# Holding each quad's load back until the quad three ahead of it has landed, in steps 5 to 12 of a graph-network layer

## The chip, the cores and the metric

One core of one Trainium2 chip runs the program. The metric is the device time of one execution in microseconds (us), and lower is better. The kernel before takes 317.98 us (median of 3 runs, 317.53 to 318.19).

## The reference

The kernel computes one pre-norm graph layer over 12,500 nodes of 128 features and 200,000 edges of 128 features, all in 32-bit floats. The edges come sorted by `dst`.

```python
h = jnp.maximum(_layernorm(x, axis=-1), 0.0)
agg = jax.ops.segment_sum(edge_attr, dst, num_segments=x.shape[0])
h = jnp.concatenate([h, agg], axis=-1)
h = jax.nn.relu(h @ W1 + b1)
h = jax.nn.relu(h @ W2 + b2)
h = h @ W3 + b3
# layer norm of h over its features, times ln_w, plus ln_b
x = x + h
```

The edge features are 102.4 MB of the 109.9 MB that are read from HBM, and each is used once.

## The kernel before, in words

**Edges.** The 200,000 rows are cut into 130 quads of 1,536 rows (`QUAD`, 768 KB each) and a small tail. A quad lies in one of the 8 slots of the tile `ring` (`RING = 8`; quad q in slot q mod 8). `load_quad` (L295) loads it with two DMAs of 384 KB, both of which raise the slot's own semaphore `edges_loaded[slot]`, by 32 in total (`LANDED`). TensorE (PE) sums a quad with 24 matmuls (`seg`, L438), which wait for that semaphore and raise `seg_done` when they are through. ScalarE copies the sums, a second matmul puts them at the right nodes (L449, with a placement matrix from GpSimd, L800), and VectorE adds them into `agg` (L954).

**Nodes.** The nodes are 32 groups of 384 and a last one of 212. One *step* i of the pipeline handles four quads (4i+6 to 4i+9) and one group's three layers. The `x` rows of group i+3 are loaded in SyncE's step i by `load_x` (L290, 192 KB).

**The order of the loads.** SyncE (SP) issues all loads of edges and x and nearly all stores, in one written order, on one DMA queue. In its step i it loads x of group i+3 and then the quads 4i+14 to 4i+17. Each goes through `reload`, which waits until the slot's previous quad has been summed:

```python
def reload(q, slot):
    sp.wait_ge(seg_done, q - RING + 1)
    load_quad(q, slot)
```

Steps 1 to 12 run in one loop over pairs of steps (L347), steps 13 to 28 in a second (L350) in which the first eight groups' results are also stored in parts (L322). After the last quad's load the other groups are stored, two at a time (L327), and the program ends with the last group's layers and stores (L758, L309, L314).

Of the kernel before, what the change touches and what calls it, by code (L numbers as in the profile page):

```python
# [39 lines left out]
LANDED = 2 * 16  # L40
# [17 lines left out]
RING = 8  # L58
# [10 lines left out]
TRIPLES = BLOCKS * BLOCK // 3 + 2  # L69
XAHEAD = 3  # L70
AHEAD = 6
OUT_PARTS = ((0, 48), (48, 96), (96, P))
STEPS = GROUPS - 1
ROUNDS = (STEPS - 3) // 2
STORED_EARLY = 8
WTS = 6 * 16


def gnn_kernel(nc, x, dst, edges, w1, b1, w2, b2, w3, b3, lnw, lnb, out):
    assert GROUPS == 32 and QUADS == 4 * STEPS + AHEAD and LAST_P * LAST_PER == LAST_N and RC * RP == REST  # L80
    with ExitStack() as ctx:
        def sb(name, shape, dt=F32):
            return ctx.enter_context(nc.sbuf_tensor(name, shape, dt))

        def sem(name):
            return ctx.enter_context(nc.semaphore(name))
# [16 lines left out]
        turn = sb("turn", [P, ROWT])  # L103
# [3 lines left out]
        row_at = sb("row_at", [P, QUADS + 1])  # L107
        rows_at = sb("rows_at", [P, AHEAD])
        excess = sb("excess", [P, 5])
# [72 lines left out]
        edges_loaded = [sem(f"edges_loaded{k}") for k in range(RING)]  # L182
# [6 lines left out]
        added = sem("added")  # L189


        dve_went_on = sem("dve_went_on")
        pool_went_on = sem("pool_went_on")

# [77 lines left out]
        with nc.Block() as block:  # L272
# [3 lines left out]
            def _(sp):  # L276
# [9 lines left out]
                def load_x(g, par, before):  # L286

                    if not (isinstance(before, int) and before == 0):
                        sp.wait_ge(x_loaded[par], 16 * before)
                    sp.dma_start(xg(g), group_rows(x, g)).then_inc(x_loaded[par], 16)  # L290

                def load_quad(q, slot):

                    for k in range(2):
                        sp.dma_start(ring_slot(slot)[:, k * HALF:(k + 1) * HALF, :], half_of_edges(q, k)).then_inc(edges_loaded[slot], 16)  # L295
# [11 lines left out]
                def store(g):  # L307
                    sp.wait_ge(out_ready, g + 1)
                    sp.dma_start(group_rows(out, g), xg(g)).then_inc(stored, 16)  # L309

                def store_last(count):
                    sp.wait_ge(out_ready, count)
                    for p0, p1 in LAST_PARTS:
                        sp.dma_start(last_rows(out, p0, p1), xg(LAST)[p0:p1, :]).then_inc(stored, 16)  # L314

                def store_part(g, k):

                    p0, p1 = OUT_PARTS[k]
                    if k == 0:
                        sp.wait_ge(out_ready, g + 1)  # L320
                    rows = out[bass.ds(g * CHUNK + p0 * PER, (p1 - p0) * PER), :]
                    sp.dma_start(rows.rearrange("(p j) f -> p (j f)", j=PER),  # L322
                                 xs[p0:p1, bass.ds(g * CHUNK, CHUNK)]).then_inc(stored, 16)

                def store_two(g):
                    sp.wait_ge(out_ready, g + 2)
                    sp.dma_start(out[bass.ds(g * CHUNK, 2 * CHUNK), :].rearrange("(g p j) f -> p g (j f)", p=P, j=PER),  # L327
                                 xs[:, bass.ds(g * CHUNK, 2 * CHUNK)].rearrange("p (g e) -> p g e", g=2)).then_inc(stored, 16)
# [5 lines that stand above are left out]
                def fast():  # L334
                    for q in range(RING, RING + AHEAD):
                        reload(q, q % RING)

                    def step(i, par, pairs, g=None, parts=()):

                        load_x(i + XAHEAD, (par + XAHEAD) % 2, pairs + (par + XAHEAD) // 2)  # L340
                        for k in range(4):
                            reload(4 * i + RING + AHEAD + k, (4 * par + AHEAD + k) % RING)
                            if k in parts:
                                store_part(g, parts[k])

                    step(0, 0, 0)
                    with sp.Fori(0, ROUNDS - STORED_EARLY) as t:  # L347
                        step(2 * t + 1, 1, t)
                        step(2 * t + 2, 0, t + 1)
                    with sp.Fori(ROUNDS - STORED_EARLY, ROUNDS) as t:  # L350
                        g = t - (ROUNDS - STORED_EARLY)
                        step(2 * t + 1, 1, t, g, {0: 0, 3: 1})
                        step(2 * t + 2, 0, t + 1, g, {2: 2})
                    sp.wait_ge(seg_done, QUADS - RING + 1)
                    tail = QUADS % RING
                    sp.dma_start(ring[:, tail, 0:PER * D],
                                 edges[TAIL0:EDGES, :].rearrange("(p j) f -> p (j f)", j=PER)).then_inc(edges_loaded[tail], 16)
                    pairs = (GROUPS - 2 - STORED_EARLY) // 2
                    for k in range(pairs):
                        store_two(STORED_EARLY + 2 * k)  # L360
                    for g in range(STORED_EARLY + 2 * pairs, GROUPS - 1):
                        store(g)
                    store_last(GROUPS)
                    singles = GROUPS - STORED_EARLY - 2 * pairs
                    sp.wait_ge(stored, 16 * (len(OUT_PARTS) * STORED_EARLY + pairs + singles + len(LAST_PARTS)))

                def general():
# [26 lines left out]
                    sp.wait_ge(stored, 16 * (GROUPS + len(LAST_PARTS)))  # L394

                branch(sp, fast, general)


            @block.tensor
            def _(pe):  # L400
# [110 lines left out]
                def fast():  # L511
                    pe.wait_ge(wts_loaded, WTS)
                    for q in range(AHEAD):
                        if q >= 2:
# [6 lines left out]
                    def step(i, par, pairs):  # L521


                        for k in range(4):
                            turn_q = 4 * par + AHEAD + k
                            q = 4 * i + AHEAD + k
# [660 lines left out]
```

## Time and profile before

| what | value |
|---|---|
| median of 3 runs | 317.98 us |
| the profiled execution: its own time | 318.58 us |
| its span, first to last instruction | 316.8 us |
| PE, DVE, ACT, POOL busy | 86%, 78%, 47%, 56% |
| mean granted TensorE clock | 0.984 |
| moved by DMA | 116.50 MB, mean 368 GB/s |

The profiled execution's own time is 1.8 us above its span, and 0.6 us above the median of the runs shown. PE is TensorE, DVE VectorE, ACT ScalarE, POOL GpSimd, SP SyncE; SPq and ACTq are the queues from which these engines issue DMAs. The time of an SPq row is the time that the issue took on SyncE, not that of the transfer. In the windows view the DMA share is the busy share of the core's 16 DMA engines; the records of neighbouring packets overlap, so that a full queue reads 1.06.

### The profile page before, as it was taken

What the parts mean: (1) busy time and instruction counts of PE and PEld (TensorE: products, weight loads), DVE (VectorE), ACT (ScalarE), POOL (GpSimd) and SP (SyncE); (2) the same over time, 40 slices, a digit from 0 to 9 for tenths busy, and PEclk for the clock granted to TensorE, in tenths of its full rate; (3) what the DMA queues carried; (4) which work ended last, traced back from release to release, by engine and by line L of the source; (5) the groups of instructions that cost most, each with busy time, mean ns of one, the idle gap of its engine ahead of it and who ended that gap; (6) DMA issues with size and microseconds to landing.
All of it is one profiled execution on the core that took longest, in us unless ns stands there. A gap on an engine that the chain in (4) does not pass through costs nothing.

```text
span 316.8 us, 12734 instructions
## 1 busy us (share of the span) xinstructions
PE 271.7 (86%) x3927; PEld 185.0 (58%) x3927; DVE 246.4 (78%) x944; ACT 149.6 (47%) x407; POOL 179.0 (56%) x208
## 2 busy tenths in 40 slices
PE   2949998998998888888988888889888888898991
PEld 0726666665665566655665565656655656565570
DVE  4946588989787878877787888778777887878885
ACT  1442555555544445455444454554443545544632
POOL 8636555566555656655555656555556565555431
PEclk9978999999999999999999999999999999999998
DMA  7999999999999999999999999999999999999994
GB/s 245 343 380 371 372 373 372 373 373 373 373 373 373 373 374 373 373 373 373 378 381 378 382 380 379 379 383 379 380 381 379 382 381 380 380 383 380 383 397 153
DMA packets 81855, 116.50 MB, mean 368 GB/s; under 512 B 5712, under 2 KB 81840, under 8 KB 81840
## 3 DMA queue, kind: packets, MB, share of 16 engines
q1 hardware_dynamic: 80826, 115.86, 103.2%
q10 hardware_dynamic: 1014, 0.46, 0.5%
q8 instruction: 7, 0.11, 0.1%
q14 instruction: 8, 0.07, 0.1%
HBM read 109.90 MB, written 6.40 MB: 367 GB/s over the span
## 4 chain that ended last, share of the span: by engine, by line
SPq 55%; PE 14%; issue 12%; DMA 11%; DVE 6%; ACT 0%; DVEq 0%; POOL 0%; POOLq 0%
SPq L295 43%; DMA ring<-in_edge_attr 9%; PE part_ps L438 6%; SPq L322 5%; SPq L290 5%; PE place_ps L449 3%; DMA dst_i<-in_dst 1%; PE hid_ps L466 1%; SPq L331 1%; PE hid_ps L483 1%; PE hid_ps L473 1%; PE y_ps L489 1%; DVE onehot L878 1%; DVE local L900 1%; DVE least L898 1%
## 5 line engine op out<-in xcount | busy, mean ns | idle before, releaser
L800 POOL TENSOR_SCALAR place<-iota,rows_at 128x128 f32<-128x128 f32 x131 | 104.9, 804 | 104.2 <-PE place_ps L449 95.0
L438 PE MATMUL part_ps<-ring,onehot 128*32 128x128 f32 x3120 | 113.4, 279 | 26.7 <-DMA ring<-in_edge_attr 25.8
L438 PEld LDWEIGHTS part_ps<-ring,onehot 128*32 128x32 f32 x3120 | 78.4, 110 | 72.6 <-issue 50.1
L954 DVE TENSOR_TENSOR agg<-place_ps,agg 128x128 f32 x131 | 38.0, 290 | 50.8 <-PE place_ps L449 49.0
L449 PE MATMUL place_ps<-place,part 128*128 128x128 f32 (+1 forms) x262 | 64.4, 328 | 2.6 <-POOL place L800 2.3
L808 POOL TENSOR_TENSOR xs<-xs,vecs 128x384 f32 (+2 forms) x33 | 54.8, 1662 | 19.4 <-ACT h L669 19.4
L878 DVE TENSOR_TENSOR onehot<-iota,local_t 128x768 f32<-128x768 f32 x66 | 63.5, 963 | 0.3 <-issue 0.3
L655 ACT ACTIVATE part<-part_ps 128x128 f32<-128x128 f32 x131 | 35.0, 268 | 48.4 <-PE part_ps L438 46.8
L449 PEld LDWEIGHTS place_ps<-place,part 128*128 128x128 f32 (+1 forms) x262 | 39.8, 190 | 29.1 <-issue 22.1
L669 ACT ACTIVATE h<-xs,x_shift,x_rstd 128x128 f32 (+2 forms) x98 | 41.3, 483 | 2.4 <-DVE x_shift L871 2.4
L685 ACT ACTIVATE hid<-hid_ps,b1s 128x384 f32<-128x384 f32 (+1 forms) x33 | 19.0, 577 | 45.4 <-PE hid_ps L473 45.4
L1013 DVE SCALAR_TENSOR_TENSOR xs<-z,y_rstd,xs 128x128 f32 (+1 forms) x93 | 32.5, 400 | 4.1
L489 PE MATMUL y_ps<-w3s,hid 128*128 128x128 f32 x192 | 29.8, 291 | 0.0
L661 ACT ACTIVATE x_std<-x_mv,eps 128x3 f32<-128x3 f32 (+1 forms) x33 | 9.8, 296 | 41.1 <-DVE x_mv L859 41.1
L995 DVE SCALAR_TENSOR_TENSOR z<-y,y_mv,vecs 128x128 f32<-128x128 f32 x96 | 28.9, 355 | 0.1
L678 ACT ACTIVATE h_t<-ht_ps 128x384 f32<-128x384 f32 x32 | 22.3, 696 | 13.6 <-PE ht_ps L458 13.6
L483 PE MATMUL hid_ps<-hid,w2s 128*128 128x384 f32 (+1 forms) x66 | 26.8, 487 | 0.5 <-ACT hid L685 0.5
L466 PE MATMUL hid_ps<-h_t,w1x 128*128 128x384 f32 x64 | 26.1, 489 | 0.8 <-ACT h_t L678 0.8
L473 PE MATMUL hid_ps<-agg,w1a 128*128 (+2 forms) x66 | 26.5, 483 | 0.0
L489 PEld LDWEIGHTS y_ps<-w3s,hid 128*128 128x128 f32 x192 | 23.8, 191 | 1.4 <-issue 0.5
L851 DVE BATCH_NORM_STATS2 x_stats<-xs 128x6 f32 (+2 forms) x98 | 22.0, 279 | 1.0 <-DVE flag_i L940 0.8
L979 DVE BATCH_NORM_STATS2 y_stats<-y 128x6 f32<-128x128 f32 x96 | 20.8, 272 | 0.1
(86 smaller groups left out, 201.9 us busy)
## 6 DMA issues: line engine op xcount, KB each, us to landing
ring<-in_edge_attr SPq DMA_DIRECT2D x260, 384.0 KB, 8.8
xs<-in_x SPq DMA_DIRECT2D x32, 192.0 KB, 8.5
out_x<-xs SPq DMA_DIRECT2D x11, 384.0 KB
out_x<-xs SPq DMA_DIRECT2D x16, 72.0 KB
dst_i<-in_dst SPq DMA_DIRECT2D x1, 768.0 KB
out_x<-xs SPq DMA_DIRECT2D x8, 48.0 KB
ring<-in_edge_attr SPq DMA_DIRECT2D x1, 192.0 KB, 8.7
out_x<-xs SPq DMA_DIRECT2D x1, 192.0 KB
```

The costliest lines, as they stand in the source:

```text
L295: sp.dma_start(ring_slot(slot)[:, k * HALF:(k + 1) * HALF, :], half_of_edges(q, k)).then_inc(edges_loaded[slot], 16)
L438: last = nc.tensor.matmul(part_ps[par_q % 2][s * WIN:(s + 1) * WIN, 0:D], onehot[:, oct_par, first + s, j, :], e[:, s, j * D:(j + 1) * D], ...
L449: nc.tensor.matmul(place_ps[par_q % 2][:, 0:P], part[0:rows, par_q % 2, :], place[0:rows, par_q % 2, :], start=True, stop=True).then_inc(p ...
L483: nc.tensor.matmul(hid2_ps[:, 0:n], w2s[:, :], hid1[:, 0:n], start=True, stop=True).then_inc(hid2_done, 1)
L489: last = nc.tensor.matmul(y_ps[:, j * D:(j + 1) * D], hid2[:, j, :], w3s[:, :], start=True, stop=True)
L655: nc.scalar.activation(part[0:rows, par_q % 2, :], part_ps[par_q % 2][0:rows, 0:D], ACT.Copy).then_inc(part_copied, 1)
L669: last = nc.scalar.activation(h[0:rows, j, :], xg(g, j), ACT.Relu, bias=x_shift[0:rows, j:j + 1], scale=x_rstd[0:rows, j:j + 1])
L800: nc.gpsimd.tensor_scalar(place[:, par_q % 2, :], iota[:, 0:P], rows_at[:, k:k + 1], None, ALU.is_equal).then_inc(place_ready, 1)
L808: nc.gpsimd.tensor_tensor(v, v, lnbs[0:rows, :].unsqueeze(1).to_broadcast([rows, per, D]), ALU.add).then_inc(x_biased, 1)
L878: nc.vector.tensor_tensor(onehot[:, par % 2, :, :, :], iota[:, 0:WIN].unsqueeze(1).unsqueeze(1).to_broadcast([P, OCT, PER, WIN]), local_t[ ...
L954: nc.vector.tensor_tensor(v, place_ps[par_q % 2][:, 0:P], v, ALU.add).then_inc(added, 1)
L1013: last = nc.vector.scalar_tensor_tensor(xg(g, j), z_of(g, j), r[0:rows, j:j + 1], xg(g, j), ALU.mult, ALU.add)
```

## The change

In SP's step, `few_underway` is called ahead of each of the four `reload`s when the step is built with `level=True`. It waits until quad q-3, counted from the quad q that is about to be loaded, has landed in full, and then raises a semaphore `sp_went_on`, for which nobody waits. The loop over steps 1 to 12 is cut in two: steps 1 to 4 as before, steps 5 to 12 with `level=True`. Everything else stays.

```diff
+UNDERWAY = 3
+LEVEL_FROM = 2
...
+        sp_went_on = sem("sp_went_on")
...
+                    def few_underway(turn, pairs):
+
+                        n = turn - UNDERWAY
+                        sp.wait_ge(edges_loaded[n % RING], LANDED * (pairs + n // RING + 1))
+                        sp.sem_inc(sp_went_on, 1)
+
-                    def step(i, par, pairs, g=None, parts=()):
+                    def step(i, par, pairs, g=None, parts=(), level=False):
 
                         load_x(i + XAHEAD, (par + XAHEAD) % 2, pairs + (par + XAHEAD) // 2)
                         for k in range(4):
+                            if level:
+                                few_underway(4 * par + RING + AHEAD + k, pairs)
                             reload(4 * i + RING + AHEAD + k, (4 * par + AHEAD + k) % RING)
...
-                    with sp.Fori(0, ROUNDS - STORED_EARLY) as t:
+                    with sp.Fori(0, LEVEL_FROM) as t:
                         step(2 * t + 1, 1, t)
                         step(2 * t + 2, 0, t + 1)
+                    with sp.Fori(LEVEL_FROM, ROUNDS - STORED_EARLY) as t:
+                        step(2 * t + 1, 1, t, level=True)
+                        step(2 * t + 2, 0, t + 1, level=True)
```

On SyncE's queue, the first half of an odd step in the loop over steps 1 to 12 before the change. `x_loaded_even` is raised by x loads, `seg_done` by PE; ISA and REGISTER_ALU rows are SyncE's own short instructions.

```order
L347 UNCONDITIONAL_BRANCH
L347 ISA
L290 ISA [waits x_loaded_even]
L290 REGISTER_ALU
L290 DMA xs<-in_x 128x384
L331 ISA
L295 ISA [waits seg_done]
L295 DMA ring<-in_edge_attr 128x2x384
L295 ISA
L295 DMA ring<-in_edge_attr 128x2x384
```

The same place of the loop over steps 5 to 12 after the change, and the start of the next quad. `edges_loaded7` and `edges_loaded0` are raised by the loads of the slots 7 and 0.

```order
L361 UNCONDITIONAL_BRANCH
L361 ISA
L293 ISA [waits x_loaded_even]
L293 REGISTER_ALU
L293 DMA xs<-in_x 128x384
L344 REGISTER_ALU
L334 ISA [waits edges_loaded7]
L298 ISA [waits seg_done]
L298 DMA ring<-in_edge_attr 128x2x384
L298 ISA
L298 DMA ring<-in_edge_attr 128x2x384
L344 ISA
```

The order of the DMAs is the same. New is the wait on the semaphore of an earlier quad's slot, ahead of the wait on `seg_done`, with two short instructions for it. Both DMAs of the quad, and all that SyncE issues later, stand behind it. The other four engines' instructions are those of before.

## Rows read from the trace of the kernel before

**Rows 1.** The page's 40 slices of the span: DMA share, and what the DMA engines moved.

```profile
DMA  7999999999999999999999999999999999999994
GB/s 245 343 380 371 372 373 372 373 373 373 373 373 373 373 374 373 373 373 373 378 381 378 382 380 379 379 383 379 380 381 379 382 381 380 380 383 380 383 397 153
```

**Rows 2.** Windows: steps without stores, steps with them.

```profile
core 0: us, PE busy (x) PEld busy (x) DVE busy (x) ACT busy (x) POOL busy (x), PEclk, DMA share, GB/s
60.00:148.00 88.00, 79.95 (x1199) 54.59 (x1201) 72.02 (x283) 44.18 (x122) 52.73 (x61) 1.00 1.06 373
150.00:290.00 140.00, 123.57 (x1843) 83.98 (x1843) 110.95 (x432) 66.56 (x183) 81.22 (x95) 1.00 1.06 380
```

**Rows 3.** Waits of PE, 60 to 148 us: in total, times, longest.

```profile
PE part_ps L438 <- DMA ring<-in_edge_attr: 8.0, 8, 1.0
```

**Rows 4.** Waits of SyncE's queue, whole span.

```profile
SPq L295 <- PE part_ps L438: 3.8, 6, 1.1
```

**Rows 5.** Timeline of SyncE's queue: start, duration; the x loads of steps 4, 5, 6, 12 and 13.

```profile
67.36 0.76 SPq L290 DMA_DIRECT2D xs<-in_x  x1
68.43 7.60 SPq L295 DMA_DIRECT2D ring<-in_edge_attr  x8
76.76 0.36 SPq L290 DMA_DIRECT2D xs<-in_x  x1
77.44 7.30 SPq L295 DMA_DIRECT2D ring<-in_edge_attr  x8
84.97 1.39 SPq L290 DMA_DIRECT2D xs<-in_x  x1
...
139.03 0.76 SPq L290 DMA_DIRECT2D xs<-in_x  x1
140.11 7.60 SPq L295 DMA_DIRECT2D ring<-in_edge_attr  x8
148.33 0.36 SPq L290 DMA_DIRECT2D xs<-in_x  x1
```

**Rows 6.** Line L295 at 60 to 148 us: issue durations (ns), issue to landing.

```profile
L295 SPq DMA_DIRECT2D ring<-in_edge_attr x80: 372/718/1484, 59.7 to 146.9; - x80
DMA to landing us min/median/max: 7.4/9.0/10.1
```

**Rows 7.** The same of L295 at 150 to 290 us and at 0 to 20 us.

```profile
DMA to landing us min/median/max: 7.0/8.8/10.5
...
DMA to landing us min/median/max: 4.7/9.7/11.3
```

**Rows 8.** Chain of waits around quad 58: start, duration.

```profile
131.21 0.04 issue
131.28 0.04 issue
131.32 0.37 SPq L295
131.70 0.04 issue
131.74 0.05 SPq L295
131.79 0.04 issue
131.86 0.04 issue
131.90 9.52 DMA ring<-in_edge_attr
```

**Rows 9.** Timeline and chain at the program's start, when the queues are empty.

```profile
0.74 0.44 SPq L278 DMA_DIRECT2D dst_i<-in_dst  x1
...
1.73 4.25 DMA dst_i<-in_dst
```

**Rows 10.** Timeline of PE, steps without stores: start, busy, idle before.

```profile
78.83 0.86 PE L438 MATMUL part_ps<-ring,onehot 128*32 128x128 f32 x24 [0.97 <-DMA ring<-in_edge_attr]
```

**Rows 11.** Windows of 2 us, columns as in rows 2.

```profile
16.00:18.00 2.00, 0.18 (x8) 0.00 (x0) 0.99 (x12) 0.88 (x2) 0.00 (x0) 1.00 1.06 386
140.00:142.00 2.00, 0.96 (x21) 0.72 (x24) 1.86 (x7) 0.82 (x2) 1.72 (x3) 1.00 1.06 373
156.00:158.00 2.00, 2.00 (x35) 1.68 (x34) 1.66 (x7) 1.76 (x6) 1.23 (x2) 1.00 1.06 388
160.00:162.00 2.00, 2.00 (x22) 0.99 (x15) 1.83 (x6) 0.28 (x1) 1.74 (x2) 1.00 1.06 372
```

**Rows 12.** DMA queues of the page: packets, MB, share of 16 engines.

```profile
q8 instruction: 7, 0.11, 0.1%
q14 instruction: 8, 0.07, 0.1%
```

## The prediction

> **What bounds the kernel now.** I read the page's slices first. The DMA engines show 9 tenths or more in every slice but the first and the last, and the rate stands at 373 GB/s through the slices in which steps 5 to 12 lie, then near 380 [rows 1]. The windows say the same with more figures: share 1.06, the reading of a full queue, and 373 GB/s between 60 and 148 us, while PE is busy for 79.95 of 88 us, DVE, ACT and POOL for less, at full granted clock [rows 2]. PE waits only for edges there: 8 times in 88 us, 8.0 us in all [rows 3], once per step, as at 78.83 us [rows 10]. So the pace of a step is that of its bytes. SyncE's timeline gives it: x loads at 76.76 us (step 5) and 148.33 us (step 13), 71.57 us for 8 steps, 8.95 us a step [rows 5]. A step moves 4 quads of 768 KB and 192 KB of x, 3,264 KB or 3.34 MB; at 373 GB/s that is 8.96 us. A quad alone is 0.786 MB and takes 2.11 us.
>
> Next, what holds SyncE back. In the whole span it waited for PE (a slot not free) 3.8 us in 6 places [rows 4]. That is not what spaces its issues. An issue takes 372 ns when nothing stops it and 718 ns in the median [rows 6]; eight of them and the x load fill about 8.4 of the 8.9 us of a step [rows 5]. The queue itself is full and holds the issue. The depth that follows from this: quad 58's halves were issued at 131.32 and 131.90 us, and the second landed 9.52 us later, at 141.42 [rows 8]. From the first issue that is 10.1 us, and 10.1 us at 373 GB/s is 3.77 MB, or 4.5 quads with their share of x. Between four and five quads are therefore underway before the change.
>
> **The change part by part.**
>
> *The new wait.* A quad q is issued when q-3 has landed, so at most two quads, q-2 and q-1, lie ahead of it instead of about four. SyncE's position slips towards the landings, from 10.1 us ahead to about three quads, 3 x 2.11 = 6.3 us (with one x load in four quads, 6.7 us on average): some 3.5 us less in store. Landings are what PE waits for, and they move only if the queue runs dry. When q-3 has landed, 2 quads or 4.2 us of work are still queued. In this time SyncE has to get past its wait and the first bytes of q have to come. SyncE's part: two or three short instructions at 0.04 to 0.08 us each, as between the rows of the chain [rows 8], say 0.3 us, and 0.37 us for the first half's issue. The rest no row shows by itself, so I bound it. From above: at the program's start, with all queues empty, 780 KB of `dst` were issued from 0.74 us on and had landed in full at 5.98 us [rows 9]. That is 5.24 us, of which the bytes take 2.14 us at 373 GB/s, so at most 3.1 us are start and completion together, the issue among them. With SyncE's 0.3 us that makes 3.4 us, against a cover of 4.2 us. From below it is the bare issue, 0.7 us. Take the upper value: 0.8 us of cover is left, and the queue does not run dry. Cost 0. If the 16 DMA engines are not level with each other, the semaphore follows the slowest, and an engine that is ahead may idle for a moment. It had its share done early, and the slowest, whose landing everybody waits for, still has its 4.2 us.
>
> By the Trainium skill (DMA: Bandwidth & Descriptors, Bandwidth and Anatomy of one DMA) a transfer costs a fixed time of about 2.0 us and then its bytes. The trace's bound of 3.1 us is larger and fits it from above; by the page's figure, an estimate, 1.9 us of cover would be left instead of 0.8. Its rule for kernel authors, to issue a DMA early and wait for it late, speaks against this change, but costs nothing here as long as that cover holds.
>
> *What is queued behind the wait.* On SyncE the x load of the next step, the other quads, and from step 13 on the first stores. Their order on the DMA queue stays word for word, so x of group i+3 still lands ahead of quad 4i+14, and VectorE gets it in the same turn. Nothing else waits for SyncE.
>
> *SyncE's own time.* It loses 8.4 us of blocked issuing per step and gets back a wait in its place. Eight issues of 0.37 us, the x load's 0.36 us and some 4 x 0.4 us of short instructions are 4.9 us of 8.95. SyncE does not become the bound.
>
> *The way in and out.* At step 5 it pauses once for about 3.5 us while the store of queued loads shrinks. At step 13 the wait ends and four free slots let it issue faster than the data land (0.37 + 0.2 us a half, against 1.05 us), so the queue fills again. Both lie beside a queue that stays busy. Cost 0.
>
> *Does a shorter queue move bytes faster?* This is where a gain could be. Within the trace of before the depth varies and the rate does not follow it. At 60 to 148 us halves land 7.4 to 10.1 us after issue, at 373 GB/s [rows 2, 6]. At 150 to 290 us they land in 7.0 to 10.5 us [rows 7], yet a window in which no store was in flight shows 372 GB/s [rows 11]. The 380 of that stage comes from windows with stores in them, such as 388 at 156 us. The one fast stretch of loads alone, 386 GB/s at 16 us, came with the deepest queue (up to 11.3 us to landing) and with compute engines nearly idle [rows 7, 11]. I take no gain.
>
> The sum is 0. The profiled execution's 316.8 us of span and 318.58 us stay as they are, and so does the median of the runs, 317.98, on which I forecast: 318.0 us.
>
> **The rivals.**
>
> *Loads run faster with less in flight.* For it: the rate is not at its ceiling, since 380 and 386 GB/s occur [rows 2, 11], and the steps in question are those with the fullest queue. Against it: the evidence above. Price: 8 steps of 3.34 MB take 71.6 us at 373 GB/s, 70.3 at 380 and 69.2 at 386, so 1.3 us, at most 2.4. Result 316.7, at the outside 315.6. The Trainium skill (DMA: Bandwidth & Descriptors, Latency and other measured facts) holds that HBM answers in 0.2 us on average and in 2 us at high load; a shorter queue would be lighter load. No row here shows latency falling with depth.
>
> *The DMA engines draw level.* If some lag behind the others, as landings that are counted by the slowest would hide, a hold that leaves the leaders idle could give the laggards a larger share of HBM, and every later quad would land earlier. The rows do not show single engines. The gain would be at most the lag that is made good: even at the rate of 380 against 373 (1.9%) over 71.6 us, 1.3 us again. It ends at the same place, 316.7. Gain and condition are close to the first rival's, and I count them together.
>
> *The queue runs dry.* The place is the wait on `edges_loaded` in each of the 32 quads. If SyncE's restart and the start of a transfer last longer than 4.2 us, three quads take that time plus their own 2.11 us instead of 6.3 us, so each us too much costs a third of a us per quad, 10.7 us in all. Against it: the bound of 3.4 us. For it: that bound comes from a core at rest, and a loaded memory may answer later; the nearest loaded rows, 7.0 us at the least to landing, contain queueing that can't be told from latency [rows 7]. From 4.2 us on it decides. At 4.5 us the result is 318.0 + 3.2 = 321.2, at 4.3 us 319.1. The far end, if the 10.1 us of quad 58 were all latency, would be (10.1 + 0.3)/3 = 3.5 us a quad instead of 2.2, +40 us; since 10.1 us is just what the 4.5 queued quads need, I leave it out.
>
> *More program to fetch.* SyncE's program grows by some 51 instructions, and another piece of it may have to be fetched through a DMA engine. The seven pieces of queue 8 are 0.11 MB, 16 KB each [rows 12]; one DMA engine moves a sixteenth of 373 GB/s, so a piece holds its engine for 0.7 us. If that is the engine that lands last, all later quads come 0.7 us later: 318.7. If it is not, nothing changes.
>
> **How the numbers follow.** No change: 0.54. Faster loads or level engines: 0.25. Queue runs dry: 0.11. A fetch on the last engine: 0.10. A measurement of this kernel tells no less than about 0.2% (0.6 us) from no change. Both kinds of the slower side end beyond that, if the fetch only just, so 0.21 slower, 0.54 same, 0.25 faster. The range goes from the first rival's 316.7 to 319.1, the small end of a dry queue; the far ends of both sides (under 316.7, over 319.1) keep the 2 in 10.
>
> **What would show it.** In the changed profile: the rate and share at 80 to 148 us (373 and 1.06 if I am right; 376 or more for the first rivals; below 370 and a share under 1.06 for a dry queue). Issue to landing of L298 there should fall from 9.0 to about 5.5 to 6 us, and its issues to the bare 0.37 us; if it stays at 9, the change does not do what it says. SyncE should wait for `ring` DMAs some 32 times. PE's waits for edges should stay one per step, about 1 us. The x load of step 13 should be issued about 3.5 us later than at 148.33 us while the landings stay where they were. I would be wrong if the pace of landings depended on how the queue is filled, in either direction.

## The result, and the profile after

The changed kernel takes 319.38 us (median of 11 runs, 318.20 to 320.74) against 318.09 us (11 runs, 317.53 to 318.84) of the kernel before. The ratio is 1.0036, 95% interval 1.0022 to 1.0049: about 1.1 us slower. A second set of 12 runs gave 1.0031 (1.0011 to 1.0051). The forecast was no change, 318.0 us, with a range up to 319.1.

The profiled execution took 318.53 us, at the low end of its kernel's runs, while that of before (318.58) lay at the high end of its own. Both spans are 316.8 us, so the spans show nothing, and the loss has to be read from stretches. First the page's slices, DMA share and GB/s.

```profile
DMA  7999999999999999999999999999999999999995
GB/s 251 327 378 377 372 374 374 373 374 373 368 367 368 370 374 373 373 373 373 377 380 378 381 381 379 379 384 378 378 383 379 379 379 382 379 381 380 380 398 185
```

Against [rows 1] four slices in the held steps fall below 373 GB/s: 368, 367, 368 and 370. They cover 79 to 111 us, the first three to four of the eight held steps. Then the rate is that of before. The windows (window in us, its length, busy time and count of each engine, granted clock, DMA share, GB/s):

```profile
core 0: us, PE busy (x) PEld busy (x) DVE busy (x) ACT busy (x) POOL busy (x), PEclk, DMA share, GB/s
84.00:100.00 16.00, 14.20 (x213) 9.89 (x213) 12.93 (x47) 7.81 (x22) 9.87 (x11) 1.00 1.04 365
100.00:116.00 16.00, 14.23 (x212) 9.86 (x212) 13.52 (x54) 8.14 (x23) 10.27 (x12) 1.00 1.06 374
116.00:148.00 32.00, 28.95 (x443) 19.62 (x441) 25.34 (x104) 16.20 (x45) 17.37 (x22) 1.00 1.06 373
160.00:280.00 120.00, 105.42 (x1576) 71.58 (x1574) 94.80 (x370) 57.26 (x157) 69.22 (x80) 1.00 1.06 380
```

The share of 1.04 where a full queue reads 1.06 says that some DMA engines had nothing to do between 84 and 100 us. 8 GB/s of 373 over 16 us is 0.34 us of moving. At 116 to 148 us, with the hold still on, share and rate are full, as in [rows 2].

SyncE does what was forecast. Its queue's waits over the whole span (in total, times, longest), its line L298 (L295 before) at 80 to 148 us, and its timeline at steps 5 and 13:

```profile
SPq L345 <- DMA ring<-in_edge_attr: 27.4, 29, 3.7
...
SPq L298 <- PE part_ps L452: 3.8, 6, 1.2
```

```profile
L298 SPq DMA_DIRECT2D ring<-in_edge_attr x62: 372/373/373, 81.0 to 147.9; - x62
...
DMA to landing us min/median/max: 4.0/5.4/6.0
```

```profile
76.42 0.36 SPq L293 DMA_DIRECT2D xs<-in_x  x1
80.96 7.71 SPq L298 DMA_DIRECT2D ring<-in_edge_attr  x8
...
151.59 0.36 SPq L293 DMA_DIRECT2D xs<-in_x  x1
```

It waits 29 times for landings, 3.7 us the first time; every issue takes the bare 0.37 us, where the median was 718 ns [rows 6]; a half lands 5.4 us after its issue instead of 9.0; the x load of step 13 goes out 3.3 us later than in [rows 5]. PE's waits for edges at 60 to 148 us look like those of [rows 3]:

```profile
PE part_ps L452 <- DMA ring<-in_edge_attr: 8.0, 9, 1.0
```

**The 16 DMA engines one by one.** A quad's landing is in the trace as 32 single events, two for each of the 16 engines (every engine carries a sixteenth of each half and reports it). No view above shows them. Worked out from the trace, for some quads, the times in us of the first event, the average of the 32, and the last, for which PE waits; levelled engines would have first and last 1.05 us apart, a half's own time:

```
               quad 33              quad 66                quad 129
before         80.97  82.66  85.02  155.28 156.95 159.26   297.06 299.10 301.88
after          81.06  82.70  84.80  156.26 157.44 158.62   298.00 299.74 301.76
```

Before the change first and last are 4.0 us apart: some engines are 3 us ahead of the slowest and stay so. Over the held stretch, quad 33 to 66, the average landing takes 74.74 us instead of 74.28: 0.46 us lost. But the last landing takes 73.81 instead of 74.24: it comes 0.4 us *sooner*. After the hold, to quad 129, the last landing takes 143.14 us, and took 142.62 before. The leaders have lost about 1 us: at quad 66 the first event is 2.4 us ahead of the last instead of 4.0.

### The profile page after: what moved, and what is told of

It is laid out like the page before. It is cut to its first block, busy times and chain, and to the rows that moved or that the text cites. A ratio compares the mean times of both kernels' runs of the same rounds, so it can differ in the third digit from the quotient of the medians.

```text
span 316.8 us, 12775 instructions
## 1 busy us (share of the span) xinstructions
PE 270.6 (85%) x3927; PEld 183.8 (58%) x3927; DVE 247.2 (78%) x944; ACT 149.3 (47%) x407; POOL 179.5 (57%) x208
## 4 chain that ended last, share of the span: by engine, by line
SPq 46%; DMA 26%; issue 12%; PE 10%; DVE 5%; ACT 1%; POOL 0%; POOLq 0%; DVEq 0%
SPq L298 34%; DMA ring<-in_edge_attr 25%; SPq L325 6%; SPq L293 4%; PE part_ps L452 4%; PE place_ps L463 2%; DMA dst_i<-in_dst 1%; SPq L334 1%; PE hid_ps L480 1%; PE y_ps L503 1%; PE hid_ps L497 1%; PE hid_ps L487 1%; DVE local L914 1%; DVE least L912 1%; DVE span L917 1%
## 5 line engine op out<-in xcount | busy, mean ns | idle before, releaser
L822 POOL TENSOR_TENSOR xs<-xs,vecs 128x384 f32 (+2 forms) x33 | 54.1, 1640 | 18.9 <-ACT h L683 18.9
L892 DVE TENSOR_TENSOR onehot<-iota,local_t 128x768 f32<-128x768 f32 x66 | 64.4, 977 | 0.3 <-issue 0.3
```

The costliest lines, as they stand in the source:

```text
L822: nc.gpsimd.tensor_tensor(v, v, lnbs[0:rows, :].unsqueeze(1).to_broadcast([rows, per, D]), ALU.add).then_inc(x_biased, 1)
L892: nc.vector.tensor_tensor(onehot[:, par % 2, :, :, :], iota[:, 0:WIN].unsqueeze(1).unsqueeze(1).to_broadcast([P, OCT, PER, WIN]), local_t[ ...
```

## The experiments

Unless told otherwise each kernel was run 12 times beside runs of the kernel before on the same chip. A single comparison resolves some 0.15 to 0.2%.

**1. The depth of the hold, and its instructions.** The changed kernel with another number in one place:

```diff
-UNDERWAY = 3
+UNDERWAY = 6
```

and likewise 4 and 2. The third run is the changed kernel unchanged. All compute everything. In the texts, theory A is that the hold leaves engines that are ahead without work, theory B that the added instructions cost the time. Theory C, from experiment 2 on, is a fixed cost of the way into or out of the hold.

> Waits for the quad six ahead (which has landed long before) instead of three, in the same steps with the same instructions. Theory A, the hold leaves DMA engines that are ahead without work and these bytes are not made good: nothing is held, so 318.1 us, the kernel before. Theory B, the added instructions or the longer program cost the time: 319.4 us, as the changed kernel.

> Waits for the quad four ahead: three quads (6.3 us) stay queued. Theory A: engines that are ahead by some 3 us still have work, 318.1 us, and the rate at 80 to 148 us stays 373 GB/s. Theory B: 319.4 us.

> The changed kernel once more, for more times and a second trace. 319.4 us, with single runs between 318.2 and 320.7. Theory A: the slices at 80 to 112 us show under 373 GB/s, deeper in a slow run than in the first trace (367 to 370). Theory B: they show 373 throughout and the time is lost elsewhere.

> Waits for the quad two ahead: one quad (2.1 us) stays queued. Theory A: most engines run dry in every quad, 2 to 6 us slower than before (320 to 324 us), rate at 80 to 148 us clearly under 373 GB/s. Theory B: 319.4 us.

Measured: six ahead 318.47 us, ratio 1.0014 (0.9998 to 1.0029); four ahead 318.34, 0.9999 (0.9984 to 1.0015); three again 318.86, 1.0031 (1.0011 to 1.0051); two ahead 335.86, 1.0550 (1.0525 to 1.0574, 5 runs). The instructions alone cost nothing that can be told with certainty, and four ahead makes 32 waits for landings at no cost either. In the second trace of three ahead two slices, from 79 to 95 us, show 367 and 354 GB/s. Four ahead, its SyncE waits and window:

```profile
SPq L345 <- DMA ring<-in_edge_attr: 24.9, 32, 1.3
```

```profile
84.00:116.00 32.00, 27.98 (x435) 19.41 (x426) 26.26 (x101) 16.31 (x46) 19.12 (x22) 1.00 1.06 373
```

Theory B falls. With two ahead the loss is 17.7 us, three times the upper end expected. Its window and its line L298:

```profile
84.00:148.00 64.00, 47.75 (x706) 31.73 (x697) 45.93 (x171) 26.47 (x74) 25.27 (x36) 1.00 0.91 304
```

```profile
L298 SPq DMA_DIRECT2D ring<-in_edge_attr x57: 372/373/373, 84.1 to 159.8; - x57
...
DMA to landing us min/median/max: 3.2/3.9/5.7
```

This is the dry queue. It also gives the price that no row of before had: a half needs 3.2 us at the least and 3.9 in the median from issue to its last landing, 1.05 of it transfer, so start and completion are 2.2 to 2.9 us for the slowest engine, with what was still queued ahead of it. The first engine is back sooner. From the landing that SyncE waits for to the first event of the new quad the trace has 2.7 to 3.7 us, 3.1 in the median; less the 1.05 us of transfer, a restart takes about 2.1 us. With one quad (2.1 us) in store nothing is left over, and the kernel loses 17.7 us over 32 quads or 0.55 us each.

**2. Where the hold stands and how long it lasts.** Steps 3 to 28 (`LEVEL_FROM = 1`, and `level=True` in the loop over steps 13 to 28 as well), steps 21 to 28 alone, and, later, steps 5 and 6 alone. The edit of the last:

```diff
-                    with sp.Fori(LEVEL_FROM, ROUNDS - STORED_EARLY) as t:
+                    with sp.Fori(LEVEL_FROM, LEVEL_FROM + 1) as t:
                         step(2 * t + 1, 1, t, level=True)
                         step(2 * t + 2, 0, t + 1, level=True)
+                    with sp.Fori(LEVEL_FROM + 1, ROUNDS - STORED_EARLY) as t:
+                        step(2 * t + 1, 1, t)
+                        step(2 * t + 2, 0, t + 1)
```

> The hold (three ahead) in steps 3 to 28 instead of 5 to 12. Theory A (bytes lost while the leading DMA engines idle are lost once, until their lead is used up, some 0.4 us, and every later event that sets one engine back costs all the others again because no lead is left as a cushion): 0.5 to 1.5% slower than before, 319.8 to 323 us, with the landings averaged over the engines later than in the changed kernel from step 13 on. Theory C (a fixed cost of the way into or out of the hold): 319.2 us, as the changed kernel.

> The hold in steps 21 to 28 only. Theory A: the rate dips by some 1.5% for three steps there, average landings 0.4 us later; the last landing of the last quads is little moved, since the engine that is behind gets a larger share during the dip. 318.2 to 319.4 us. Theory C: 319.2 us.

> The hold in steps 5 and 6 only. If the loss is made once, in the first quads of the hold, the average landing is 0.3 to 0.45 us later from step 7 on and the time is that of the changed kernel, +0.2 to +0.4%. If it grows with the number of held quads, a quarter of it is left, under 0.1%.

Measured: steps 3 to 28 319.34 us, 1.0046 (1.0024 to 1.0069); steps 21 to 28 319.51, 1.0036 (1.0016 to 1.0057); steps 5 and 6 319.20, 1.0032 (1.0012 to 1.0053). Two held steps cost what eight cost. The average landing from quad 33 to 66 took 74.88 us with two held steps (0.59 more than before), all of it by quad 50. So what is lost in the hold is lost once, in the first quads, and does not grow with the length of the hold. The first run lies below its expected 319.8; its interval reaches past that and does not tell it from the changed kernel. Theory A also wanted its average landings to fall further behind after step 13, and they do not: quad 66 to 129 took 142.50 us on average, within the changed kernel's 142.30 to 142.81. A hold that goes on is no dearer than one that ended. The second run lies just above theory A's 319.4. In its trace the average landing is 0.4 us late at quad 124, as expected, but the last landing, 0.25 us early there, is 1 us late at quad 125, which was not. The times of the three runs alone would fit theory C as well; what goes beyond it comes from the single events and from experiment 5.

**3. One engine set back ahead of the hold.** A load of 37 rows of 1.5 KB, which one DMA engine carries out alone, after step 0, in the kernel before and in the changed one:

```diff
                     step(0, 0, 0)
+                    sp.dma_start(extra[0:37, :], x[0:111, :].rearrange("(p j) f -> p (j f)", j=PER)).then_inc(extra_loaded, 16)
```

> The kernel before with one more load of 37 rows of 1.5 KB (57 KB of x into a tile that nobody reads), which a single DMA engine carries out, after step 0. It sets that engine back by some 2.4 us. If single engines keep their lag to the end, the last landings come up to 2.4 us later and the time is 319 to 320.6 us; if the 16 engines share their work, 0.2 us later, 318.3 us.

> The changed kernel with the same load of 37 rows on one engine. Prediction's view (an engine that is ahead idles at no cost): the same as lag_only. Theory A: the other engines idle in step 5 and after until the lag is down to some 1.4 us, the rate at 84 to 116 us falls well below the 369 GB/s of the changed kernel (to 340 to 360), the average landing is 1.5 to 3 us later than in lag_only, while the last landing gains at most 1 us on it: 0 to 1% slower than lag_only.

Measured: without the hold 318.40 us, 1.0012 (0.9997 to 1.0027); with it 319.68, 1.0055 (1.0039 to 1.0070, 6 runs). The setback alone costs next to nothing: quad 33's last landing is 2.4 us behind the average, as without it, so the engine that got it was not the last, and its lead took it up. The held kernel was expected to drop to 340 to 360 GB/s and did not:

```profile
84.00:100.00 16.00, 14.35 (x213) 10.03 (x213) 12.95 (x47) 7.85 (x22) 9.84 (x11) 1.00 1.04 365
```

365 GB/s is the changed kernel's own figure. The average landing from quad 33 to 66 took 74.72 us, 0.4 more than without the hold, as in the changed kernel. The experiment did not make the last engine later, so it says nothing on a larger lag of that one. That part of the expectation is a miss.

**4. More traces of the changed kernel.**

> The changed kernel, another trace. About one run in four was 1.5 to 2.5 us above the others. If such a run is caught, its trace shows a stretch of half clock for PE after a wait for the late quads near 293 us, as in the trace of hold_late; if instead it shows full clock, the slow runs come from the landings alone.

> The changed kernel, a fourth trace. If a run above 320 us is caught: half clock for PE near 295 us if the clock is its cause, full clock and a later last landing if the landings are. A run under 319 us shows neither.

Measured: single runs of 320.18 and 319.06 us. Both show full clock between 30 and 310 us. In the first, quad 41 landed 2.86 us after quad 40 instead of 2.11, within the held stretch, and quad 66 landed 3.29 us after quad 65, 0.7 us more than in the first trace, when an 8 KB packet of queue 14 (program) had just held one engine. At the x load of 156.2 us the last engine is 0.92 us behind the average of the 16, at that of 165.4 us it is 1.60, and the other 15 have moved by at most 0.1. The last landing of quad 129 stands at 302.74 us, 1.0 us later than in the first trace. So 1.0 of the 1.65 us by which this run is longer are in its landings; the rest lies behind the last quad, and none of it comes from a lower clock before 310 us.

With these there are six traces with the hold in step 5 and after (three of experiments 1 and 4, the first one, and `hold_steps_5_6` and `lag_hold3`) and four without any effective hold (before, six ahead, four ahead, `lag_only`). Durations between landings in us, from the same single events, as averages over the traces:

```
                                 4 without   6 with    difference
quad 33 to 66, average landing     74.31      74.83      +0.53
quad 33 to 66, last landing        74.22      74.04      -0.19  (five of six: -0.38 to -0.52)
quad 66 to 129, average landing   142.27     142.57      +0.30
quad 66 to 129, last landing      142.09     143.31      +1.22
quad 33 to 129, last landing      216.32     217.35      +1.03
```

The last row is of the size of the measured slowdown, about 1.1 us. Not all of it is the hold's doing: at quad 33, before the hold can act, the last engine of the six happened to be 0.4 us closer to the average (2.05 us behind it, against 2.41), so that at quad 129 they are 0.6 us later by the clock, and their own times are 0.7 us longer. The second and fourth rows say where the last landing falls behind: not in the hold, but after it. Of the 1.22 us, 0.54 come bit by bit up to quad 124, 0.43 at quad 125 and 0.25 after that. The first and third rows are the other side of the account: the average landing is 0.83 us late over the whole stretch, and at quad 129 the last engine is as far behind the average with the hold (2.0 us) as without (2.2). What the idle leaders did not move is missing in the end.

**5. One engine set back after the hold.** The open question was what happens after it. A load of 29 rows, again carried out by one engine, this time between steps 12 and 13 in both kernels. At a sixteenth of 373 GB/s the 44.5 KB hold it for 1.9 us.

```diff
+                    sp.dma_start(extra[0:29, :], x[0:87, :].rearrange("(p j) f -> p (j f)", j=PER)).then_inc(extra_loaded, 16)
                     with sp.Fori(ROUNDS - STORED_EARLY, ROUNDS) as t:
```

> The kernel before, with a load of 29 rows of 1.5 KB (44 KB, read by nobody) that a single DMA engine carries out, issued between steps 12 and 13. It sets this engine back by 29 packets, some 1.9 us. Cushion theory: the engine is ahead of the last one by 1 us or more, so the last landing moves by under 1 us from quad 66 to 90; the time rises by 0 to 0.9 us over the kernel before.

> The changed kernel with the same load of 29 rows at the same place, after the hold has ended. Cushion theory: the hold has used up the lead, so the last landing moves by 0.4 us or more beyond what it moves in setback_before, and the time is 1.0 to 2.0 us above setback_before (the changed kernel alone was 1.0 above the kernel before). If no cushion matters and the loss is the bytes of the hold alone: 0.5 to 1.0 us above setback_before, with equal moves of the last landing.

Measured: without the hold 318.32 us, 1.0010 (0.9995 to 1.0026); with it 320.40, 1.0063 (1.0043 to 1.0083, 6 runs). The same 44.5 KB cost 0.3 us in the one, which is not told from nothing, and about 1 us more than the hold itself in the other. PE's timeline at quad 66, first without, then with the hold:

```profile
159.80 0.86 PE L442 MATMUL part_ps<-ring,onehot 128*32 128x128 f32 x24 [1.07 <-DMA ring<-in_edge_attr]
```

```profile
162.15 0.86 PE L456 MATMUL part_ps<-ring,onehot 128*32 128x128 f32 x24 [2.63 <-DMA ring<-in_edge_attr]
```

PE waits 1.07 us at this quad, its usual wait of a step, and 2.63 us with the hold. The last landing from quad 63 to 70 takes 16.17 us against 15.92 in the kernel before (+0.25), and 17.71 against 16.02 in the changed one (+1.69). The x loads around it, 16 events each, show the engine itself. With the hold the 15 others stay within 0.7 us of the average and one goes from at most 0.64 us behind it, at 148.6 us, to 2.15, at 157.8 us. Without the hold the last engine is 1.95 us behind the average ahead of the setback and 1.91 after it: the one set back comes in ahead of it. The setback is the same; the lead that took it up is gone. One thing more is in the second trace. It came into the hold with a larger lag, 3.4 us from average to last at quad 33 (2.1 in the changed kernel's first trace), and its window shows what that costs:

```profile
84.00:100.00 16.00, 14.16 (x212) 9.73 (x210) 13.51 (x55) 8.14 (x23) 10.41 (x12) 1.00 1.01 345
```

345 GB/s instead of 365, and 2.3 us of average landing lost from quad 33 to 50 instead of 0.4. Part of this run's time belongs to that and not to the setback, so the step in PE's wait is the clean figure, not the total.

## Why the prediction was wrong

**What bounds the kernel, the depth, SyncE's part: right.** 373 GB/s away from the dip, bare issues of 0.37 us, 29 waits (some 32 were forecast), 5.4 us to landing (5.5 to 6), SyncE 3.3 us later at step 13 (3.5).

**The cover of 4.2 us: right for the slowest engine, and for it alone.** The bound of 3.1 us for start and completion held: 2.2 to 2.9 us were measured with two ahead, and a restart of about 2.1 us for the first engine. Three quads ahead, nothing shows the slowest engine dry: the last landing kept its pace in every held quad but those with an event of their own.

**The step that failed** is the one behind the cover: an engine that is ahead "may idle for a moment. It had its share done early", cost 0. The leaders were 2.5 to 3 us ahead in the six traces, so of the 4.2 us in store they had 1.2 to 1.7, and a restart takes 2.1 us or more. They ran dry, and at quad 50 the first event came 0.9 to 1.2 us later for it (by the sum, 0.4 to 0.9). Their idling loses bytes (0.4 to 0.8 us of average landing, share 1.04), and it is true that this does not delay the last landing then and there: this came 0.4 us sooner in five of six traces. What the prediction did not see is what the lead was worth. It is a cushion. Every time one engine is set back, the quad is late only if that engine is or becomes the last. With leads of up to 3 us most setbacks are swallowed, and with the lead used up they are handed on. Experiment 5 shows it for a setback made by hand. So the share that was "done early" is not free: the average landing of experiment 4 ends 0.8 us late.

That the kernel has such setbacks of its own is in every trace: a 16 KB packet of queue 8, program being fetched [rows 12], which holds one engine for 1.1 us near 290 us. Quad 125, the next to land, came 2.0 to 2.1 us after quad 124 in four of five traces without the hold (2.85 in the fifth, the kernel before). In nine of the ten traces with one, two ahead included, it came 2.2 to 3.5 us after it. The tenth is `setback_hold3` with 2.02: there one engine was already far behind, and the others had a lead on it again. That this packet is what makes quad 125 late was not tried; the time, the size and the difference between the two groups fit, and so do the x loads: in the changed kernel the last engine is 0.90 us behind the average at 282.7 us and 1.61 at 291.8 us. What makes the last landing fall behind bit by bit between quads 66 and 124, 0.54 us on average, stays open.

**The rivals.** The engines do draw level, as the second rival had it, and the sign of its first half was right (0.4 us sooner). It stopped at the end of the hold and missed the price. Faster loads with less in flight: refuted, since four ahead, with 8.0 us to landing instead of 9, ran at 373 GB/s and 318.34 us, and three ahead moved 373 GB/s at 116 to 148 us with 5.4 us to landing. The dry queue is real one step further, at two ahead, at 0.55 us a quad. The fetch of program is not what costs: queues 8 and 14 show 7 and 8 pieces as before, but one of the 8 KB pieces is now fetched in mid-stream, at 156.38 us, and holds its engine for 0.35 us. Six and four ahead have it too, at 153.19 and 154.88 us, and they are not slower. A piece of 16 KB holds its engine for 1.1 us, not the 0.7 that the prediction took.

**The range** ended at 319.1 for a dry queue of all engines; a partly dry one, of the leaders, gave 319.4. The rows that I had, a landing counted by its slowest engine, could not tell how far the engines were apart, and that was taken as a reason to price it at nothing rather than as a cost to be bounded.

No version that beats both kernels came out of this. The hold with four ahead is the kernel before within 0.15%.

## What to carry to other kernels

A transfer that is spread over several DMA engines lands with its slowest one, but the lead of the others is not slack to be given away: it takes up what later happens to single engines. Before a queue is made shorter, look at how far the engines are apart, not only at the share and the rate, and leave each of them more in store than a restart takes (here up to 3 us of lead and a restart of 2.1 us, an estimate of 5.1 us together: four quads ahead left 6.3 us in store and were free, three left 4.2 and cost 0.3%, two left 2.1 and cost 5.5%). And when two spans agree, compare the stretches and the medians before calling it no change.

## What the runs showed of the hardware

The 16 engines keep their distances to 0.01 us over 72 us of loads alone: in the kernel before, the x loads of 73.6 and 145.3 us show the same 16 offsets, 0 to 3.00 us. In this stretch no lag is worked off. With stores among the loads, from 154 to 281 us, single distances move by up to 0.5 us, while first and last stay 3.0 us apart.

The last engine runs a little faster while the leaders idle: quads without an x load between them landed 2.00 to 2.08 us apart instead of 2.11 in the first held steps.

In the trace of `hold_late` PE's granted clock fell from 2.4 to 1.2 GHz for 3.4 us from 295.1 us on. Ahead of that it had waited 1.43 us for quad 125, and it was in a wait of 0.77 us for ScalarE when the clock fell. Window and timeline:

```profile
291.00:299.00 8.00, 5.80 (x64) 3.63 (x63) 5.83 (x20) 3.73 (x12) 3.19 (x4) 0.79 1.04 360
```

```profile
293.02 0.86 PE L453 MATMUL part_ps<-ring,onehot 128*32 128x128 f32 x24 [1.43 <-DMA ring<-in_edge_attr]
...
295.40 1.65 PE L481 MATMUL hid_ps<-h_t,w1x 128*128 128x384 f32 x2 [0.77 <-ACT h_t L693]
```

The same two matmuls took 0.91 us in the changed kernel, after 0.80 us of waiting for quad 125 and the same 0.77. That execution took 320.83 us, and 17.1 us from the last quad's landing to the end of the span instead of 14.5 to 15.7 in all other traces. It is one trace, and that the late quad brought the lower clock is not shown; it suggests that a late quad near the end can cost more than its own lateness.
